# Six row sums of squares moved from TensorE to GpSimd and VectorE, in a quantised feed-forward kernel

## The reference

```python
# layer 0: RMS norm with a conditioned scale, GELU-gated feed-forward, quantised down projection
scale = cond @ norm_w.T + 1.0
ms = jnp.mean(x * x, axis=-1, keepdims=True)
h = x * (scale[:, None, :] * rsqrt(ms + EPS))
val, gate = jnp.split(h @ up_w.T, 2, axis=-1)
h = val * gelu(gate)
y = act_quant(h) @ weight_quant(down_w).T + x
# layer 1: adapter whose weights come from the condition
Wd_b = Wd + (cond @ Wdd.T + bdd) * 0.1
Wu_b = Wu + (cond @ Wdu.T + bdu) * 0.1
out = y + relu(y @ Wd_b.T + bd) @ Wu_b.T + bu
```

## Time and profile before

| | |
|---|---|
| median of 3 runs | 850.98 us (849.87 to 851.22) |
| span of the profiled execution | 847.8 us; its own time with what lies around the span is not listed apart |
| granted TensorE clock | 1.000 (2.4 GHz) over the span |
| TensorE busy | 98% |
| VectorE busy | 71%; 80% to 100% in most slices up to about 320 us |
| ScalarE busy | 46% |
| GpSimd busy | 9%: 64 tensor operations until 168 us, 8 all-reduces |
| DMA | 216 GB/s mean, up to 385 GB/s in single quads of super-block 1 |

### The profile page before, as it was taken

The page is one execution under the profiler, slowest core; times in us unless marked ns, Lnnn a source line. Parts: engine busy times, 40 slices in busy tenths (PEclk is TensorE's granted clock), DMA queues, the critical chain, the costliest instruction groups (busy, mean ns, idle before and its releaser), DMA issues.

```text
span 847.8 us, 11801 instructions
## 1 busy us (share of the span) xinstructions
PE 834.7 (98%) x3982; PEld 366.9 (43%) x3982; DVE 605.6 (71%) x904; ACT 388.4 (46%) x633; POOL 74.3 (9%) x79
## 2 busy tenths in 40 slices
PE   6999999999999999999999999999999999999998
PEld 4334444444444444444444444444444444444443
DVE  5998787989877765658776656668975664445986
ACT  5778887775454532237454542126333332224000
POOL 0363332202000000002000000000200000000100
PEclk9999999999999999999999999999999999999999
DMA  9879988665999843377889754436246444432232
GB/s 342 333 269 339 348 285 300 235 224 209 323 350 373 305 149 117 116 255 274 294 308 335 270 200 134 151 106 211 84 133 217 137 162 141 140 117 77 99 123 76
DMA packets 64426, 183.49 MB, mean 216 GB/s; under 512 B 7024, under 2 KB 8304, under 8 KB 64368
## 3 DMA queue, kind: packets, MB, share of 16 engines
q1 hardware_dynamic: 64080, 182.48, 61.7%
q10 hardware_dynamic: 288, 0.26, 0.1%
HBM read 152.31 MB, written 29.36 MB: 214 GB/s over the span
## 4 chain that ended last, share of the span: by engine, by line
PE 93%; DVE 1%; issue 0%; DVEq 0%
PE aux_ps L1182 10%; PE b_ps L1082 9%; PE b_ps L1086 9%; PE b_ps L1084 9%; PE a_ps L1082 6%; PE a_ps L1086 6%; PE a_ps L1084 6%; PE aux_ps L1137 6%; PE aux_ps L1233 3%; PE aux_ps L1224 3%; PE c_ps L1086 3%; PE c_ps L1082 3%; PE c_ps L1084 3%; PE e_ps L1082 3%; PE e_ps L1086 3%; PE e_ps L1084 3%
## 5 line engine op out<-in xcount | busy, mean ns | idle before, releaser
L1590 DVE SCALAR_TENSOR_TENSOR h_ring<-v_sb,unscale,gelu 128x512 f32<-128x512 f32 x63 | 50.9, 808 | 101.2 <-ACT gelu L885 53.4
L861 ACT ACTIVATE b_ps<-a_ps 128x512 f32<-128x512 f32 x63 | 36.7, 583 | 140.4 <-PE a_ps L1086 140.3
L1082 PE MATMUL b_ps<-t_mov,u_l 128*128 128x512 f16 x252 | 95.5, 379 | 0.6 <-DVE c_ps L1551 0.6
L1086 PE MATMUL b_ps<-t_mov,u_l 128*128 128x512 f16 x252 | 95.5, 379 | 0.0
L1084 PE MATMUL b_ps<-t_mov,u_l 128*128 128x512 f16 x252 | 95.5, 379 | 0.0
L1614 DVE TENSOR_TENSOR hmax<-gelu,hmax 128x512 f32<-128x512 f32 x120 | 82.8, 691 | 7.6 <-ACT gelu L891 2.5
L1182 PE MATMUL aux_ps<-h_ring,wq 128*128 128x512 f16 x384 | 84.8, 379 | 0.0
L753 POOL PARTITION_ALL_REDUCE yscale<-hmax x8 | 17.9, 2266 | 601.3 <-DVE hmax L1614 600.7
L895 ACT ACTIVATE gelu<-h_ring 128x512 f32<-128x512 f32 x64 | 40.3, 630 | 56.5 <-DVE h_ring L1590 56.5
L891 ACT ACTIVATE gelu<-h_ring 128x512 f32<-128x512 f32 x64 | 40.2, 629 | 52.5 <-DVE h_ring L1600 52.4
L1600 DVE SCALAR_TENSOR_TENSOR h_ring<-b_ps,unscale,gelu 128x512 f32<-128x512 f32 x64 | 47.9, 749 | 18.9 <-PE b_ps L1086 18.7
(11 more groups left out here) (225 smaller groups left out, 1620.0 us busy)
## 6 DMA issues: line engine op xcount, KB each, us to landing
w_ring<-in_Wdu SPq DMA_DIRECT2D x64, 512.0 KB, 6.1
w_ring<-in_Wdd SPq DMA_DIRECT2D x56, 512.0 KB, 6.9
u_l<-ul_dram SPq DMA_DIRECT2D x48, 512.0 KB, 4.5
u_e<-ue_dram SPq DMA_DIRECT2D x48, 384.0 KB, 3.1
h_ring<-in_up_w SPq DMA_DIRECT2D x16, 512.0 KB, 6.7
x_sb<-in_x SPq DMA_DIRECT2D x8, 1024.0 KB, 8.0
res<-in_down_w SPq DMA_DIRECT2D x16, 512.0 KB, 7.1
ul_dram<-u_l SPq DMA_DIRECT2D x15, 512.0 KB, 5.6
```

Of the source, the lines that this page charges most:

```text
L1082: pe.matmul(ps[:, :], weight(n, p, 0, k), hi, start=fresh and k == 0, stop=False, skip_group_check=True)
L1086: mm = pe.matmul(ps[:, :], weight(n, p, 1, k), hi, start=False, stop=k == 1, skip_group_check=True)
L1590: dve.scalar_tensor_tensor(out=h_slot(n)[:, TB:TS], in0=val[:, :], scalar=unscale[:, s // 2, j:j + 1], in1=gelu2[:, :], op0=ALU.mult, op1= ...
```

## The change

The four matmuls of `stat(i)` for i = 2 to 7 are gone, and with them the wait of product 5 for `mean_square` and the semaphore `s_stat`. GpSimd gets a new `square_total(i)`: an all-reduce with addition of `res[:, 2, :]` into `res[:, 3, :]`, so that each partition holds all 512 column sums. VectorE multiplies that by a 128 x 128 identity laid over each of the four groups of 128 tokens, and reduces each group along the free dimension; so partition p holds the sums of tokens p, 128 + p, 256 + p and 384 + p, where `stat` had put them. Blocks 0 and 1 stay on TensorE, and so does `spread_rs`.

```diff
+TOTAL_BEHIND = {7: 2, 10: 3}
...
+        square_grid = res[:, 3, :].rearrange("p (t q) -> p t q", t=NT)
+        diagonal = ident[:, :].unsqueeze(1).to_broadcast([P, NT, P])
...
+            def square_total(i):
+
+                pool.wait_ge(s_sqp, (KD - 1) * (i - 1))
+                pool.partition_all_reduce(res[:, 3, :], res[:, 2, :], P, AR.add)\
+                    .then_inc(s_square_total, 1)
+
             pool.wait_ge(s_rs, 2)
             for j in SUM_ORDER:
                 weight_sums(j)
-            for n in range(NP, NQ, NP):
-                all_h(n // NP - 1)
+                if j in TOTAL_BEHIND:
+                    square_total(TOTAL_BEHIND[j])
+            for s in range(1, NSB):
+                all_h(s - 1)
+                if s + 1 < NSB:
+                    for t in range(2):
+                        square_total(2 * s + 2 + t)
             all_h(NSB - 1)
...
                 if k == 0 and i % 2:
-                    act.wait_ge(s_stat, i - 2)
+                    act.wait_ge(s_square_total, i - 2)
+                if k == 1 and i % 2:
+                    act.wait_ge(s_ms, i)
...
-                    if stat_of_quad(n - 1) is not None:
-                        pe.wait_ge(s_ms, stat_of_quad(n - 1) + 1)
...
-                if stat_of_quad(n) is not None:
-                    pe.wait_ge(s_p5sb, n)
-                    stat(stat_of_quad(n))
...
                 elif i:
-                    dve.wait_ge(s_stat, i - 1)
-                    total = e_ps[:, 2:2 + NT]
+
+                    dve.wait_ge(s_square_total, i - 1)
+                    total = ms_half[:, col:col + NT]
+                    link(dve.tensor_tensor(square_grid, square_grid, diagonal, ALU.mult))
+                    link(dve.tensor_reduce(total, square_grid, AX_X, ALU.add))
```

More of the change, by code:

```diff
@@ L417, in build @@
         s_spread = sem("s_spread")
+        s_square_total = sem("s_square_total")
         s_xs = sem("s_xs")
@@ L435, in build @@
         s_down_total = sem("s_down_total")
-        s_stat = sem("s_stat")
         s_stage = sem("s_stage")
@@ L1140, in adapter_group, with stat0 @@
                 mm.then_inc(s_aux, 1)
[L1142 to L1149, removed]
+            def stat0():
+                ps = take("stat", 0)
+                pe.wait_ge(s_sqr, KD - 1)
+                sq = h_ring[:, 0, 0:TB]
                 for t in range(NT):
@@ L1152, in stat @@
                                    start=True, stop=True)
-                mm.then_inc(s_stat if i else s_aux, 1)
+                mm.then_inc(s_aux, 1)
             def stat1(part):
@@ L1247, in _ @@
             pe.wait_ge(s_const, 1)
-            stat(0)
+            stat0()
             stat1(0)
```

## The result

The changed kernel takes 854.44 us (854.13 to 854.90, 4 runs) against 850.42 us (849.67 to 851.22, 4 runs) of the kernel before. The ratio is 1.0052, with a 95% interval of 1.0038 to 1.0067. The forecast was 845.7 us, in a range of 844.3 to 849.0. The span of the profiled execution is 852.3 us, 4.5 us more than before; 854.75 us is that execution's own time.

A forecast was written before the change was run, and what follows sets the result against it. TensorE, busy 834.7 of 847.8 us, was taken to bound the kernel; 5.3 us off its queue and nothing back from VectorE or GpSimd gave 850.98 - 5.3 = 845.7 us, range 844.3 to 849.0.

The forecast's parts named there:

- the removal gives 5.3 us: TensorE's queue: six stats gone give 0.89 us in quad 6, 0.79 in quad 9, 3.60 in the four later ones.
- VectorE's part: Heads of six quads: product 0.68 us and reduction 0.65, 1.4 us a block with gaps, 8.4 in all, all covered.
- The all-reduce at 2.3 us: GpSimd: six adding all-reduces of 128x512 at 2.3 us each, like the trace's eight maxima, within 6.9 to 11 us of room.
- 0.97: VectorE beside an all-reduce: one all-reduce costs it up to 0.97 us, against 1.61 us idle afterwards in quad 22.
- the prediction's other price: Quad 6, by the skill's port-lock rule: VectorE could lose 2.3 us, passing on some 0.8, for a gain of 4.5.
- GpSimd's queue: Super-block 0: weight sums queued behind the all-reduce; step 8's shift to about 95.0 to 98.7, 6 us before ScalarE's use.
- the third rival: GpSimd's queue: a long adding all-reduce holds VectorE, 864.7 us at 15 us each; repeated setup over 6 us delays weight sums; 0.10.
- the chance of slower: Probability that the changed kernel measures slower, through the all-reduce on GpSimd: 0.10.
- the first change only: GpSimd behind step 7's weight sums: first-call setup of about 6 us, just hidden by 6.82 us of idle time.
- Nothing is gained: TensorE: what it saves comes back as waits for loads, DMA being nearly full in super-block 1; 851 us, chance 0.09.
- VectorE becomes late: Quads 6, 7 and 10: a dearer reduction or blocking takes 1.9 to 4 us back; about 848.3 us, chance 0.14.
- its second mechanism: GpSimd set up again at each change between tensor operations and all-reduces; if over 6 us, weight sums come late.

The follow-up runs named there:

- Experiment 3: Kernel before the change, with the six stats of blocks 2 to 7 left out and nothing in their place: 845.24 us, ratio 0.9941.
- experiment 1: Changed kernel with only blocks 4 to 7 summed by GpSimd and VectorE, blocks 2 and 3 back on TensorE: 846.02 us, ratio 0.9946.
- experiment 6: Changed kernel without VectorE's product with the diagonal and reduction; mean square takes four columns of the all-reduce's result: 856.40 us, ratio 1.0068.
- experiment 9: Kernel of experiment 1 with a maximum of absolute values in place of the addition in its four all-reduces: 846.47 us in one run.
- experiment 4: Kernel before the change plus two unneeded 128x4 all-reduces on GpSimd, behind the weight sums of steps 7 and 10: 852.10 us, ratio 1.0027.
- experiment 2: Changed kernel with only blocks 2 and 3 on GpSimd and VectorE, blocks 4 to 7 on TensorE: 858.56 us, ratio 1.0091.

## Why the prediction was wrong, by its own steps

**TensorE bounds, and the removal gives 5.3 us: right.** Experiment 3 gives 5.15, and in the traces quad 22's stat gives 0.90, quad 6's 0.89 and quad 9's 0.81.

**VectorE's part: right in size and in cost.** The groups of the changed kernel (busy, mean ns):

```profile
L1478 DVE TENSOR_REDUCE ms_half<-res 128x4 f32<-128x512 f32 x6 | 4.1, 686 | 0.2
L1477 DVE TENSOR_TENSOR res<-res,ident 128x512 f32<-128x512 f32 x6 | 4.1, 684 | 0.0
```

0.65 and 0.68 were taken, and it stayed covered (experiments 1 and 6).

**The all-reduce at 2.3 us: wrong in size, without effect in the late blocks.** It takes 3.25 us in super-block 0 and 4.14 later; in the late blocks experiment 9 puts 1.3 us of that on the addition. There it slows VectorE's two quantising products from 2.35 to 4.40 us, 2.05 and not 0.97, but not the 4.14 that a block for its whole length would take. The 1.6 us of idle time and the room behind it took it up, as experiment 1 shows. The squares of block 4 are in fact added up at 257.88 and wanted at 269.07 in the kernel before, a quad earlier than the prediction read, with the same 11 us between. In quad 6 the prediction's other price doesn't follow from its own terms: 2.3 us lost against 0.8 of room pass on 1.5, not 0.8. The trace can't decide it, as the all-reduce came at 94.50, when `seed_c` had already begun at 94.13.

**The step that failed is GpSimd's queue.** "Those of step 8 run from 92.23 to 95.96; behind the all-reduce they run from about 95.0 to 98.7. ScalarE uses them at 105.15, 6 us later." I counted the all-reduce's own 2.3 us and nothing for the way into it and back. They ran from 105.30 to 108.18, and ScalarE's use moved from 105.15 to 106.91. The two configuration rows stood in the earlier trace rows, and the third rival said that being set up at each change, for over 6 us, would make weight sums late. But I put it behind the length of the all-reduce, in one rival at 0.10, and priced only the latter. The mechanism was named and its price was not worked out. It could have been bounded: the trace of before had one change, under 33 us of idle time, so its cost lay anywhere from nothing to 33 us; and the new order has four of them between operations whose users left 6 us and 5 us. With that bound the chance of slower could not stay at 0.10.

The Trainium skill, GPSIMD Engine Reference, "Instruction dispatch", has about 6 us at the first call of a newly loaded kernel. I used it for the first change only, where the 6.82 us of idle time would hide it. In these traces the idle time at a change that waits for nothing else is 6.1 to 11.4 us, and the way back to tensor operations costs it as well.

**Rivals.** *Nothing is gained* fell with experiment 3, *VectorE becomes late* with 6; VectorE is late in quads 8 and 11, but as a link in GpSimd's chain. Of the third rival the named cause, a long all-reduce that holds VectorE, did not come; its second mechanism did.

## What to carry to other kernels

On GpSimd, count changes of kind before operations: an all-reduce between tensor operations costs the way in and the way back, together 15 to 22 us here, with an all-reduce of 0.44 us as with one of 3.25. Put all-reduces where one change serves all of them, or where nothing behind them in GpSimd's queue is due for some 25 us. And where a trace shows a step only under a long idle time, its price is unknown, not zero: take the idle time as its upper bound, and see what the new place leaves.

## What the runs showed of the hardware

- Configuration instructions stand at each change between tensor operations and all-reduces, in both directions. The idle time with them, where nothing else released GpSimd, was 9.2, 7.6 and 10.4 us in the changed kernel, 10.2, 11.4, 6.1 and 8.6 in experiment 4, and 10.8, 6.8 and 10.4 in experiment 2. What its length depends on was not tried, and what GpSimd does in it no trace shows.
- An all-reduce of 128x512 took 2.84 us with a maximum and 4.14 with an addition, in the same place. VectorE's two products beside it took 3.33 and 4.40 us, against 2.35 without.
- After TensorE's standstill of 3.68 us, which followed one of 1.01, the granted clock was 0.50 for some 5.3 us of work; after 1.77 us, in the same trace, it stayed at 1.00. The length of the last standstill alone doesn't decide: after 2.58 us in experiment 6 and 2.91 in experiment 4 the clock fell, after 2.64 in experiment 2 it did not.
